# One statistics round for both halves of the first stage, products read in step order, and batch norm sums taken from the scaled product

## The reference

```python
x = x + conv3x3_per_channel(ln_c(x), kernel)              # layer norm over the 64 channels, eps 1e-6
t = to_tokens(x)                                          # 65536 tokens of 64 channels
Wx = ln_t(t) @ W.T                                        # layer norm over the channels, eps 1e-5
Wx = (Wx - mean(Wx)) * rsqrt(var(Wx) + 1e-5) * gamma + beta   # batch norm over all tokens of both images
y_n = sigmoid(Wx_n + y_{n-1} @ V.T)                       # a scan along the tokens
t = t + y
...                                                       # linear attention, then a mixture of experts
```

## Time and profile before

| | us |
|---|---|
| median of three runs | 1916.01 (1915.69 to 1917.2) |
| span of the profiled execution | 1912.9 |
| first add of POOL in the first stage to the end of its last finish | 44.0 to 728.6 |
| batch norm block, from its first DVE instruction | 758.0 |
| second stage, from its first transfer | 765.1 |

### The profile page before, as it was taken

The page is one execution under the profiler, slowest core; times in us unless marked ns, Lnnn a source line. Parts: engine busy times, 40 slices in busy tenths (PEclk is TensorE's granted clock), DMA queues, the critical chain, the costliest instruction groups (busy, mean ns, idle before and its releaser), DMA issues. The chain is left out here.

```text
span 1912.9 us, 24349 instructions
## 1 busy us (share of the span) xinstructions
PE 1553.3 (81%) x5627; PEld 645.6 (34%) x5627; DVE 1437.4 (75%) x2312; ACT 1238.2 (65%) x2178; POOL 1466.9 (77%) x1086
## 2 busy tenths in 40 slices
PE   3899999999999994598877478999999999924300
PEld 1333333333333331265554233333333333203200
DVE  1679999999999986398887647999999999971000
ACT  2777777777777761388866358888888988620000
POOL 2999999999999992058787319999999999911475
PEclk8999999999999997799989789999999999965555
DMA  4578888888888764989997526888888888652011
GB/s 149 167 226 249 254 245 246 249 253 249 244 246 255 209 199 132 289 298 368 372 390 304 220 45 189 284 285 278 276 283 289 281 288 251 193 171 57 1 2 2
DMA packets 111406, 429.81 MB, mean 225 GB/s; under 512 B 44672, under 2 KB 47648, under 8 KB 66208
## 3 DMA queue, kind: packets, MB, share of 16 engines
q1 hardware_dynamic: 91376, 423.77, 69.7%
q10 hardware_dynamic: 16432, 4.29, 1.3%
q0 software_dynamic: 3456, 0.19, 0.2%
HBM read 257.89 MB, written 170.01 MB: 224 GB/s over the span
## 5 line engine op out<-in xcount | busy, mean ns | idle before, releaser
L454 ACT ACTIVATE tap_products<-xn,kk 128x512 f32<-128x512 f32 x384 | 275.0, 718 | 158.5 <-POOL x_and_products L485 152.8
L485 POOL TENSOR_TENSOR x_and_products<-tap_products,x_and_products 128x512 f32<-128x512 f32 x256 | 327.2, 1278 | 41.2 <-POOL x_and_products L485 3.5
L385 PE MATMUL pst<-xn,taps 128*128 128x512 f32 x768 | 351.5, 593 | 0.0
L1495 POOL TENSOR_SCALAR exp_q<-exp_q 128x512 f32<-128x512 f32 x128 | 189.6, 1481 | 71.8 <-ACT exp_q L1446 71.8
L913 DVE SCALAR_TENSOR_TENSOR pss<-region,bn,pss 128x256 f32<-128x256 f32 x432 | 195.8, 488 | 64.2 <-PE pss L807 61.9
L852 POOL TENSOR_TENSOR x_block<-x_block,region 128x2048 f32<-128x2048 f32 x28 | 155.3, 5545 | 110.8 <-ACT region L839 83.2
L543 DVE SCALAR_TENSOR_TENSOR pst<-xn,kk,pst 128x512 f32<-128x512 f32 x256 | 191.9, 750 | 60.5 <-PE pst L385 60.3
L385 PEld LDWEIGHTS pst<-xn,taps 128*128 128x128 f32 x768 | 145.6, 190 | 186.7 <-issue 186.7
L1490 POOL TENSOR_TENSOR sq_norm<-x_ring 128x512 f32<-128x512 f32 x128 | 188.6, 1474 | 6.6 <-DVE x_ring L1542 2.7
L485 POOL TENSOR_TENSOR x_and_products<-tap_products,x_ring 128x512 f32<-128x512 f32 x128 | 163.7, 1279 | 19.7 <-ACT tap_products L454 19.7
L425 ACT ACTIVATE sq<-x_ring 128x512 f32<-128x512 f32 x256 | 157.6, 622 | 17.1 <-POOL x_ring L492 10.1
(11 more groups left out here) (246 smaller groups left out, 2970.0 us busy)
## 6 DMA issues: line engine op xcount, KB each, us to landing
rstd_wide<-rstd_scratch SPq DMA_DIRECT2D x128, 512.0 KB, 7.2
x_ring<-in_x SPq DMA_DIRECT2D x32, 1024.0 KB, 5.3
x_scratch<-x_ring SPq DMA_DIRECT2D x32, 1024.0 KB, 4.3
xl_scratch<-wx SPq DMA_DIRECT2D x32, 1024.0 KB, 8.7
region<-xl_scratch SPq DMA_DIRECT2D x32, 1024.0 KB, 11.4
x_ring<-x_scratch SPq DMA_DIRECT2D x32, 1024.0 KB, 5.7
rstd_of_channels<-rstd_scratch SPq DMA_DIRECT2D x64, 512.0 KB, 7.3
out<-x_ring SPq DMA_DIRECT2D x32, 1024.0 KB, 6.8
```

The costliest lines, as they stand in the source:

```text
L385: m = pe.matmul(wide(pst[g % 2]), taps[:, n * P:(n + 1) * P], tap_rows(g, t), start=(n == 0), stop=(n == len(PE_TAPS) - 1))
L454: act.activation(prod[:, n, :, :], tap_rows(g, t), ACT.Copy, scale=kk[:, t:t + 1]).then_inc(products, 1)
L485: pool.tensor_tensor(xr[:, g % XR, :], prod[:, n, :, :].rearrange("p r w -> p (r w)"), xr[:, g % XR, :] if n else x_tile(g), ALU.add).then ...
L1495: pool.tensor_scalar(e, e, 1.0, None, ALU.min).then_inc(clipped, 1)
```

## The change

1. One statistics round n serves block n of the first half and block n - 4 of the second. The weights are two 128 x 32 matrices (`stat_of`), each with columns for one half only, so that both halves' means accumulate in one PSUM tile; the eps is a column with a value for each partition. `STATS` becomes (0, 16), and `SQ1`, `PROJECT` and `SCALE` get two more steps of lag. SP writes and spreads the results of both halves at one place.
2. PE reads x1 and its squares in step order (`by_step`: neighbouring columns lie 16 elements apart) for the second half's statistics and for `project`. The spread result and the product are then in step order, and `scale_wx` writes runs of 32 elements.
3. `scale_wx` also sums its output for each tile (`accum_out`), and ACT squares u and sums the squares (`square_u`). `statistics` is gone; the batch norm block sums the 128 numbers of each kind, with one small product instead of two.
4. The taps are shared out anew, in a cycle of four tiles (`taps_of`): PE 3, 2, 3, 2; DVE 3, 4, 4, 4; ACT and POOL 3, 3, 2, 3. Variance and clamp move within DVE's step, the load of x comes one step later (-7 for -8).

```diff
-            SQ, CENTER, TAPS, SUMS, FINISH, SQ1, PROJECT, SCALE = -4, 5, 8, 9, 10, 10, 18, 19
-            STATS = (0, 14)
+            SQ, CENTER, TAPS, SUMS, FINISH, SQ1, PROJECT, SCALE = -4, 5, 8, 9, 10, 12, 20, 21
+            STATS = (0, 16)
+            BEHIND = (STATS[1] - STATS[0]) // TPB
...
+            def taps_of(g):
+                return ((PE_TAPS, [6, 7, 8], [0, 1, 2]),
+                        (PE_TAPS[:2], [5, 6, 7, 8], [0, 1, 2]),
+                        (PE_TAPS, [2, 6, 7, 8], [0, 1]),
+                        (PE_TAPS[:2], [5, 6, 7, 8], [0, 1, 2]))[g % 4]
...
+            def norms_in(n):
+                return [(l, n - BEHIND * l) for l in range(2) if 0 <= n - BEHIND * l < NBLK]
+            def by_step(row):
+                return row.rearrange("p (c n) -> p n c", n=CLEN)
...
-                def rstd_to_dram(l, k):
-                    n = round_of[l, k]
+                def rstd_to_dram(n):
                     sp.wait_ge(rstd_ready, n + 1)
-                    for b in range(B):
-                        sp.dma_start(rstd_d[l][k, b, :].rearrange("(j n) -> j n", n=TILE),
-                                     rstd[16 * b:P:32, n % 2, :]).then_inc(rstd_out[n % 2], 16)
+                    for l, k in norms_in(n):
+                        for b in range(B):
+                            sp.dma_start(rstd_d[l][k, b, :].rearrange("(j n) -> j n", n=TILE),
+                                         rstd[16 * l + 8 * b:P:32, n % 2, :]).then_inc(rstd_out[n % 2], 16)
...
-                    for l in range(2):
-                        if (k := block_at(t, STATS[l] + 2)) is not None:
-                            rstd_to_dram(l, k)
-                        if (k := block_at(t, STATS[l] + 3)) is not None:
+                    if (n := round_at(t, 2)) is not None:
+                        rstd_to_dram(n)
+                    if (n := round_at(t, 3)) is not None:
+                        for l, k in norms_in(n):
                             rstd_to_channels(l, k)
...
-                    if (k := block_at(t, -8)) is not None:
+                    if (k := block_at(t, -7)) is not None:
                         load(k)
...
+                    for l, k in norms:
+                        for j in range(TPB):
+                            x_in = by_step(x_tile(TPB * k + j)) if l else x_tile(TPB * k + j)
+                            m = pe.matmul(psm[32 * j:32 * j + 32, :], stat_of[:, l, :], x_in,
+                                          start=(l, k) == norms[0], stop=(l, k) == norms[-1])
                     m.then_inc(mean_ready, 1)
...
-                    pe.matmul(psw[g % 2][:, :], wcT[:, :], x_tile(g), start=True, stop=True).then_inc(wx_ready, 1)
+                    pe.matmul(psw[g % 2][:, :], wcT[:, :], by_step(x_tile(g)), start=True, stop=True).then_inc(wx_ready, 1)
...
+                def square_u(g):
+                    act.wait_ge(u_ready, g + 1)
+                    if g:
+                        act.wait_ge(u_squared, g)
+                    act.activation(u_squares[:, :].rearrange("p (n c) -> p n c", n=CLEN), u_steps(g), ACT.Square,
+                                   accum_out=sums[:, 1, g:g + 1]).then_inc(u_squared, 1)
...
-                    dve.tensor_tensor(by_chunk, psw[g % 2][:, :].rearrange("p (c n) -> p c n", n=CLEN),
-                                      rb[1][:, k % 2, cols_of(g % TPB)].rearrange("p (c n) -> p c n", n=CLEN),
-                                      ALU.mult).then_inc(u_ready, 1)
-
-                def statistics(g):
-                    dve.wait_ge(u_ready, TPB * (g // TPB + 1))
-                    dve.bn_stats(stats[:, g, :], u[:, g // TPB % 2, cols_of(g % TPB)]).then_inc(bn_done, 1)
+                    dve.scalar_tensor_tensor(out=u_steps(g), in0=stepped(psw[g % 2][:, :]), scalar=1.0,
+                                             in1=stepped(rb[1][:, k % 2, cols_of(g % TPB)]), op0=ALU.mult, op1=ALU.mult,
+                                             accum_out=sums[:, 0, g:g + 1]).then_inc(u_ready, 1)
...
-                    for l, k in rounds:
-                        variance(l, k)
                     if g is not None:
                         tap(g, 1)
-                    if (g2 := tile_at(t, SCALE + TPB)) is not None:
-                        statistics(g2)
-                    for l, k in rounds:
-                        clamp(l, k)
+                    if n is not None:
+                        variance(n)
+                    if g is not None and last == 3:
+                        tap(g, 2)
+                    if n is not None:
+                        clamp(n)
                     if g is not None:
-                        tap(g, 2)
+                        tap(g, last)
...
-                dve.bn_aggr(bn[:, 0:2], stats[:, :, :].rearrange("p t n -> p (t n)")).then_inc(step, 1)
+                dve.tensor_reduce(bn[:, 0:2], sums[:, :, :], AX.X, ALU.add).then_inc(step, 1)
```

More of the change, by code:

```diff
@@ L64, in constants @@
     start = np.arange(P)[:, None] * N
-    return np.concatenate([eye, mean, eye - mean, heads, pair, base, iota] + later + [start], 1).astype(np.float32)
+    eps = np.where(np.arange(P)[:, None] % 32 < 16, EPS_C, EPS_T)
+    return np.concatenate([eye, mean, eye - mean, heads, pair, base, iota] + later + [start, eps], 1).astype(np.float32)
 def build_program(nc, x, conv_k, ffn_w, ffn_v, gamma, beta, q_w, q_b, kv_w, kv_b, proj_w, proj_b,
@@ L209, in _ @@
                     dve.tensor_copy(stat32[:, 16 * b:16 * b + 16], meanm[:, b * C:b * C + 16]).then_inc(copied, 1)
+                    for l in range(2):
+                        dve.tensor_copy(stat_of[:, l, 16 * l + 8 * b:16 * l + 8 * b + 8],
+                                        meanm[:, b * C:b * C + 8]).then_inc(copied, 1)
                 dve.wait_ge(transposed, 9)
@@ L222, in build_program @@
             XR = 3
-            NP, ND = len(ACT_TAPS), len(DVE_TAPS)
+            NP = 3
+            def taps_of(g):
[3 more added lines that the diff above has]
+                        (PE_TAPS[:2], [5, 6, 7, 8], [0, 1, 2]))[g % 4]
+            dve_taps, act_taps = ([sum(len(taps_of(i)[who]) for i in range(g)) for g in range(NT + 1)] for who in (1, 2))
             X = sb("x_ring", [P, XSLOTS, BLOCK], F32, ph)
@@ L280, in block_at, with round_at @@
                 return k if rest == 0 and 0 <= k < NBLK else None
+            def round_at(t, lag):
+                n, rest = divmod(t - lag, TPB)
+                return n if rest == 0 and 0 <= n < ROUNDS else None
             def cols_of(s):
@@ L450, in tap_product @@
                             act.wait_ge(halo, halos[g + 1])
-                    if g >= 1:
-                        act.wait_ge(product_added, NP * (g - 1) + n + 1)
-                    t = ACT_TAPS[n]
-                    act.activation(prod[:, n, :, :], tap_rows(g, t), ACT.Copy,
+                    q, t = act_taps[g] + n, taps_of(g)[2][n]
+                    if q >= NP:
+                        act.wait_ge(product_added, q - NP + 1)
+                    act.activation(prod[:, q % NP, :, :], tap_rows(g, t), ACT.Copy,
                                    scale=kk[:, t:t + 1]).then_inc(products, 1)
                 for t in range(SQ, STEPS_A):
-                    for l in range(2):
-                        if (k := block_at(t, STATS[l] + 2)) is not None:
-                            rsqrt(l, k)
+                    if (n := round_at(t, 2)) is not None:
+                        rsqrt(n)
                     g = tile_at(t, TAPS)
@@ L463, in _ @@
                         tap_product(g, 0)
-                    for l in range(2):
-                        if (k := block_at(t, STATS[l])) is not None:
-                            square_mean(l, k)
+                    if (n := round_at(t, 0)) is not None:
+                        square_mean(n)
                     if g is not None:
-                        tap_product(g, 1)
-                        tap_product(g, 2)
+                        for n in range(1, len(taps_of(g)[2])):
+                            tap_product(g, n)
                     if (g := tile_at(t, SQ)) is not None:
@@ L473, in _ @@
                         square(1, g)
+                    if (g := tile_at(t, SCALE + 2)) is not None:
+                        square_u(g)
             @blk.gpsimd
@@ L498, in _ @@
                     if (g := tile_at(t, TAPS)) is not None:
-                        for n in range(NP):
+                        for n in range(len(taps_of(g)[2])):
                             add_product(g, n)
@@ L512, in norm_x @@
                         dve.wait_ge(taps_ready, done)
-                        dve.wait_ge(products, NP * done)
-                        dve.wait_ge(acc_step, ND * done)
+                        dve.wait_ge(products, act_taps[done])
+                        dve.wait_ge(acc_step, dve_taps[done])
                     ps, scale = wide(psc[g % 2]), rb[0][:, k % 2, cols_of(g % TPB)].rearrange("p (r w) -> p r w", w=W)
@@ L627, in _ @@
```

(6 more changed lines are left out.)

129 lines of the change are left out of this document (69 added, 60 removed).

## The result

The changed kernel takes 1999.84 us (median of four runs, 1997.1 to 2000.33) against 1916.61; the ratio is 1.0429, 95% interval 1.0417 to 1.0442. The forecast was 1869 us, with 1920 as the upper end. The time went where the first rival had put it, reads in step order that cost PE more; the number that came near, about 1990 us, stood there for another mechanism.

What follows compares the result with a forecast made beforehand. POOL was taken to set the first stage's pace, with PE right behind. 32 blocks x -1.34 = -42.9, +0.5 setup, -1.3 drain, -3.3 batch norm block: -47.0 us, giving 1869 us; own range 1862 to 1880, 8-in-10 range 1860 to 1920.

Steps and rivals of the forecast that it cites:

- the first rival: PE's projections and second-half statistics: step-order reads cost PE more, making the kernel slower, about 1930 or 1990 us; chance 0.18.
- the price of PE's read in step order: Four projections and two quads a block: 0.4 to 2.9 us more, PE 19.6 to 22.1; lower end taken.
- milder form: First rival with DVE's 57% on PE's six slots: PE needs 22.1 us a block, about 1930 us.
- harsher form: First rival if a quad's four streams lose their side-by-side run: 3.44 us a quad, +5.2 a block, about 1990 us.
- the loop of the round: Small writes, broadcasts, scaling, variance, exponential: 19.5 to 20.7 us a block, taken as hidden; as second rival 1889 us, chance 0.20.
- POOL's floor: POOL in the first stage: one add fewer a block, 21.32 - 1.34 = 19.98 us, setting the pace.
- the drain: After the last finish: the four scalings each get 0.33 us shorter, -1.3 us; added lag costs only its own work.
- PE's 22 slots: PE per block: taps from 12 to 10, 22 x 0.86 + 0.3 = 19.2 us if step-order products cost like contiguous ones.
- The batch norm block: Seam after the first stage: aggregation becomes a sum, one product goes, one one-column operation is added; -3.3 us.
- the setup: Start of the first stage: four more small copies on DVE at 0.12 us each, +0.5 us.
- The scaling with its sum: DVE's scaling writes runs of 32 and also sums; priced as a tap, 0.75 us, 0.33 less each.
- The third rival: ACT, held by the four quads at one place, leaves POOL without products: no change, about 1915 us; chance 0.04.

Runs made afterwards that it cites:

- token order: Against the changed kernel: PE reads all its products contiguously again, DVE's scaling writes u scattered, shared round and sums stay; 1906.77 us, ratio 0.995.
- the kernel with 8 bytes: Against the changed kernel: PE's reads 2 elements instead of 16 from column to column, leaving out the right token order in u; 1898.2 us, one run.
- the cut: Against the kernel with PE in token order: variance and clamp of a round moved ahead of the scaling in DVE's step; 1861.56 us, ratio 0.9722.

## Why the prediction was wrong

**The step that failed** is the price of PE's read in step order: "I take the lower end". It was 5.2 us a block, where I had allowed 0.4 to 2.9. Both ends were made of percentages, POOL's 8% and DVE's 57%, carried over to an engine with another pace. Nothing in the trace said that a percentage carries over. By the column, POOL takes 2.5 ns (1278 ns for 512) and 2.7 strided, DVE 1.3 ns contiguous and 2.0 to 2.1 strided, a pass of PE 0.84 ns and in step order 1.66. Neither the percentage nor the time of a strided column is the same on the three, but the engine with the shortest column pays the largest share. Had I put DVE's 2.1 ns on PE's passes as the upper end, it would have read 2.15 us a slot, some 7.7 us a block, and would have held the measured 1.70; that one bound would have held here is no rule. The number 0.84 ns stood in the prediction, as an argument for the cheap end; it should have been one for doubt.

**The first rival** was right in its main claim, and its signs came: slots beyond 1.1 us, PE without gaps, POOL waiting for DVE's `acc`. I gave it 0.18. Its milder form, 1930 us with DVE's 57%, was too low. It gave about 1990 us in its harsher form, for four streams of a quad that lose their side-by-side run. That form's sum of 5.2 us a block is the one measured, by chance: the quads keep running side by side at half pace (1.78 us, not 3.44), and it is the four projections, which I had held for safe, that bring 3.4 of the 5.2.

**The second step that failed**, hidden by the first, is the loop of the round. I added it up to 19.5 to 20.7 us and took it as hidden. In token order it is 21.1, above POOL's floor and above my upper end; with the contiguous scaling that I had assumed it is 20.95, in the kernel with 8 bytes. The place was right: broadcast, scaling, and the variance behind it in DVE's queue. The term that was too small is the transfers: from the first broadcast's issue to the last landing I had 2.5 + 9.5 = 12.0 us, and it is 13.2. In the drain the loop does the same once more. With it, the last round's variance waits for the broadcast of the round before: 37.9 us from the last finish to the batch norm block in the changed kernel, 36.6 in token order, 28.4 with the cut, 29.4 before. I had -1.3.

**What held.** POOL was the bound before, and its floor with one add fewer is 19.9 us a block (19.98 forecast). PE's 22 slots and three taps more on DVE fit under it: the kernel with contiguous reads and the loop cut takes 1861.56 us, 7 under the 1869 (the first stage up to the last finish gains 47.4 us there, where 42.9 were forecast). The batch norm block gave 3.7 us back (3.3 forecast), the setup 0.2 to 0.6 (0.5). The scaling with its sum takes 0.69 + 0.08 us (0.75). The third rival did not come: where PE and the loop are out of the way, POOL waits for nothing. The later stages did not change in the changed kernel (1148.4 us against 1147.8); in the profiled execution of the cut, the shortest of its four, they take 1141.2 us, for which nothing in the edit gives a reason.

## What to carry to other kernels

Do not carry the price of an access pattern from one engine to another as a percentage, least of all to a faster one: here POOL at 2.5 ns a column paid 8%, and PE at 0.84 ns paid double. Where no row shows the pattern on the engine at hand, the range must take in the rival, or a small run must price it first. Before moving a stride from one engine to another, ask which of the two is nearer to its limit; here DVE had room for 0.35 us a tile, and PE had not for 0.84. Where a queue holds a wait for a transfer ahead of work that the next such transfer needs, add up the whole loop, and try the other order in the queue first: here it was worth 45 us once PE was out of the way, and 2 us before.

## What was not expected of the hardware

PE's fp32 product takes 0.86 us with columns 4 bytes apart, 0.90 at 8, 1.78 at 16 and 1.70 at 64, at a granted clock of 1.00 in all four. Four products side by side on 32 columns each, with four strided streams at once, pay the same factor as one (1.78 against 0.88). DVE pays 1.03 us for 0.69 with one strided operand in SBUF, and no more with a second one in PSUM.
